# Two of the eight key tiles' maxima laid into the score banks by ScalarE instead of multiplied in by TensorE

## The reference

```python
attn = jnp.einsum('bhqd,bhkd->bhqk', attn_q, attn_k) / math.sqrt(HD)
rel = (pos[None, :] - pos[:, None]).astype(x.dtype)
attn = attn + slopes[None, :, None, None] * rel[None, None, :, :]
attn = jax.nn.softmax(attn, axis=-1)
out = jnp.einsum('bhqk,bhkd->bhqd', attn, v)
```

## Time and profile before

| What | Value |
|---|---|
| median of 3 runs | 1104.69 us (1103.84 to 1105.12) |
| the profiled execution's own time | 1104.65 us |
| its span in the trace | 1102.8 us |
| TensorE busy | 1050.2 us, 95% of the span |
| VectorE busy | 825.1 us, 75% |
| GpSimd busy | 791.3 us, 72% |
| ScalarE busy | 712.9 us, 65% |
| global attention, first to last score product | 103.5 to 684.6 us of the span |

### The profile page before, as it was taken

One profiled execution on the slowest core, in us unless ns is written; L12 is line 12 of the kernel. 1 busy time (PEld: TensorE's weight loads), 2 busy tenths in 40 slices (PEclk: granted clock), 3 DMA queues, 4 the chain that ended last, 5 costly groups with the idle time before them and its releaser, 6 DMA issues. The chain is left out here.

```text
span 1102.8 us, 23118 instructions
## 1 busy us (share of the span) xinstructions
PE 1050.2 (95%) x8304; PEld 652.5 (59%) x8304; DVE 825.1 (75%) x1490; ACT 712.9 (65%) x1285; POOL 791.3 (72%) x542
## 2 busy tenths in 40 slices
PE   7985999999999999999999999889999897999988
PEld 3662555555555555555555555766777694777778
DVE  7975676767666666666666664689999689999876
ACT  3663676767676767676767665048877656888754
POOL 3873678778777877787778778679996338666526
PEclk9995999999999999999999999999999999999999
DMA  8697123204132232141322100101111100111111
GB/s 267 212 285 235 37 50 78 58 30 107 30 79 58 59 78 59 31 106 34 83 57 51 39 13 21 39 11 33 34 44 35 25 2 17 36 35 34 36 29 34
DMA packets 71744, 71.70 MB, mean 65 GB/s; under 512 B 31396, under 2 KB 56528, under 8 KB 71632
## 3 DMA queue, kind: packets, MB, share of 16 engines
q1 hardware_dynamic: 71632, 70.23, 24.0%
HBM read 44.65 MB, written 15.85 MB: 55 GB/s over the span
## 5 line engine op out<-in xcount | busy, mean ns | idle before, releaser
L923 DVE CUSTOM_DVE_ANT_0 junk<-psum,alibi 128x1024 bf16<-128x1024 f32 x256 | 312.7, 1222 | 194.2 <-PE psum L995 186.5
L888 ACT ACTIVATE E<-psum,keybias_sb 128x1024 f32<-128x1024 f32 x256 | 277.8, 1112 | 189.6 <-PE psum L1019 175.2
L805 POOL TENSOR_TENSOR sum_p<-sum_p,E 128x1024 f32<-128x1024 f32 x96 | 232.8, 2425 | 84.4 <-ACT E L888 79.8
L1031 PE MATMUL psum<-E,V 128*64 128x512 f32 x1024 | 248.0, 605 | 0.0
L995 PE MATMUL psum<-KH,QH 64*128 64x512 f32 x512 | 118.6, 459 | 11.6 <-PEq L292 6.0
L1031 PEld LDWEIGHTS psum<-E,V 128*64 128x64 f32 x1024 | 62.1, 136 | 112.3 <-issue 106.4
L995 PEld LDWEIGHTS psum<-KH,QH 64*128 64x128 f32 x512 | 49.4, 189 | 120.5 <-DVE M L923 84.2
L1019 PE MATMUL psum<-QH,KH 64*128 64x512 f32 x512 | 102.2, 395 | 2.2 <-DMA QM<-mrow 2.2
L813 POOL TENSOR_TENSOR sum_p<-sum_p,xpos_sb 128x1024 f32<-128x1024 f32 x32 | 76.5, 2390 | 38.2 <-DVE xpos_sb L933 38.2
L1019 PE MATMUL psum<-QL,KH 64*128 64x512 f32 x512 | 101.5, 392 | 0.0
L1019 PE MATMUL psum<-QH,KL 64*128 64x512 f32 x512 | 101.4, 392 | 0.0
(11 more groups left out here) (155 smaller groups left out, 2087.2 us busy)
## 6 DMA issues: line engine op xcount, KB each, us to landing
qa_scratch<-tQ SPq DMA_DIRECT2D x8, 1024.0 KB, 5.3
QH<-qa_scratch SPq DMA_DIRECT2D x32, 256.0 KB, 3.6
QH<-qa_scratch SPq DMA_DIRECT2D x64, 128.0 KB, 3.5
vp_att<-v_att SPq DMA_DIRECT2D x64, 128.0 KB, 2.3
XF<-inverse_scratch SPq DMA_DIRECT2D x30, 256.0 KB, 3.4
KH<-k_scratch SPq DMA_DIRECT2D x16, 256.0 KB, 4.2
KL<-k_scratch SPq DMA_DIRECT2D x16, 256.0 KB, 5.2
v_scratch<-v_sb SPq DMA_DIRECT2D x16, 128.0 KB, 4.5
```

The source lines that it names most:

```text
L805: pool.tensor_tensor(sum_p[:, s, :], first, E[:, k % 4, :], ALU.add)\
L888: act.activation(E[:, k % 4, :], scores(k % 2), ACT.Exp, bias=kb).then_inc(exp_done, 1)
L923: dve.tensor_tensor_reduce(junk[:, :], banks(max_bank(i, k), 2), alibi[:, s, :], -1.0, BIG, ALU.add, ALU.min, M[:, s, k:k + 1]).then_inc(m ...
L1031: last = pe.matmul(banks(6 + i % 2)[HD * ch:HD * ch + HD, :], V[:, g, k, :], E[:, k % 4, ch * 512:(ch + 1) * 512], start=(k == 0), stop=(k ...
```

## The change

In heads 1 to 30, for key tiles 5 and 7 (`LAID`), the fourth product is left out. In its place ScalarE copies a wide tile, `m_wide` (128 partitions that each hold all 1024 negated maxima of the head), into the score banks, right after the exponential of tile `k - 2` (`lay_m`); TensorE waits for that copy (`laid_done`), and all three products that are left accumulate onto it. The wide tile is made by two new DMAs for each such head: `put_m` writes `mrow` to DRAM, `widen_m` reads the row back into all partitions. `put_m` stands between `load_m` and `widen_inverse` in SyncE's queue, `widen_m` after `spread_denominators`. `m_wide` lies in the first half of `XF`; for that `den_sb` moves to a buffer of its own, and the users of this half of `XF` at the end of the stage wait for the last laying. `take_m` also waits for `put_m` of the row's use two heads ago. `alibi_row` moves from after tile 5 to after tile 7.

```diff
@@ -96,6 +96,7 @@
     k_d = nc.dram_tensor("k_scratch", (B, KV // 2, 2, P, TB, P), F32, kind="Internal").ap()
     v_d = nc.dram_tensor("v_scratch", (B, P, TB, KW), F32, kind="Internal").ap()
     inv_d = nc.dram_tensor("inverse_scratch", (2, N), F32, kind="Internal").ap()
+    m_d = nc.dram_tensor("maxima_scratch", (2, N), F32, kind="Internal").ap()
 
     with ExitStack() as whole:
         whole.enter_context(nc.allow_non_contiguous_dma(reason="a few columns of biases"))
@@ -664,9 +665,10 @@
 
             sum_p = sb("sum_p", [P, 2, N])
             sum_d = xpos[:, 1].rearrange("p t s q d -> p (t s q d)").rearrange("p (s n) -> p s n", n=N)
-            den_sb = XF[:, 0:DQ // P, :].rearrange("p t d -> p (t d)")
+            den_sb = sb("den_sb", [P, DQ])
             inv_wide = XF[:, TB:T, :].rearrange("p t d -> p (t d)")
             inv_rows = XF[:, 4:8, :].rearrange("p t d -> p (t d)").rearrange("p (s n) -> p s n", n=DQ)
+            m_wide = XF[:, 0:TB, :].rearrange("p t d -> p (t d)")
             den8 = sb("den8", [P, 2, TB])
             inv8 = sb("inv8", [P, 2, TB])
             ones = sb("ones_m", [P, 32])
@@ -694,11 +696,24 @@
             inv_done = sem("inv_done")
             wide_mm = sem("wide_mm")
             o_done = sem("o_done")
+            m_out = sem("m_out")
+            m_in = sem("m_in")
+            laid_done = sem("laid_done")
             NP, ND = len(POOL_SUMS), len(DVE_SUMS) - 1
 
 
             def scores(s):
                 return banks(2 * s, 2)
+
+            LAID = (5, 7)
+
+            def is_laid(i, k):
+
+                return k in LAID and 0 < i < HEADS - 1
+
+            def laid_before(i):
+
+                return len(LAID) * (min(i, HEADS - 1) - 1)
 
             LEAD = TB + TB // 2
 
@@ -724,6 +739,18 @@
                         for ch in range(2):
                             sp.dma_start(QM[HD * ch:HD * ch + 1, s, :].bitcast(F32).rearrange("p (t c) -> p t c", c=P),
                                          mrow[TB // 2 * ch:TB // 2 * (ch + 1), s, :].bitcast(F32)).then_inc(ld_m[s], 16)
+
+                    def put_m(i, s):
+
+                        need(sp, mrow_done, i + 1)
+                        need(sp, m_in, 16 * (i - 2))
+                        sp.dma_start(m_d[s].rearrange("(t c) -> t c", c=P), mrow[:, s, :].bitcast(F32)).then_inc(m_out, 16)
+
+                    def widen_m(i, s):
+
+                        need(sp, m_out, 16 * i)
+                        need(sp, laid_done, laid_before(i))
+                        sp.dma_start(m_wide, m_d[s].partition_broadcast(P)).then_inc(m_in, 16)
 
                     def spread_denominators(i, s):
 
@@ -769,10 +796,14 @@
                             put_inverse(i - 2, i % 2)
                         if i + 1 < HEADS:
                             load_m(i + 1, (i + 1) % 2)
+                        if i + 1 < HEADS - 1:
+                            put_m(i + 1, (i + 1) % 2)
                         if i > 1:
                             widen_inverse(i - 2, i % 2)
                         if 0 < i < HEADS - 1:
                             spread_denominators(i - 1, (i - 1) % 2)
+                        if i + 1 < HEADS - 1:
+                            widen_m(i + 1, (i + 1) % 2)
 
                     for i in range(HEADS):
                         head(i)
@@ -825,6 +856,7 @@
                         head(i)
                     divide(HEADS // 2 - 2)
                     second_rstd(pool, 0)
+                    pool.wait_ge(laid_done, laid_before(HEADS - 1))
                     for t in range(NORMED):
                         modulate_out(pool, t)
                         shifted_out(pool, t)
@@ -866,7 +898,14 @@
                     def take_m(i, s):
                         need(act, m_turned, i + 1)
                         need(act, ld_m[s], 32 * (i // 2))
+                        need(act, m_out, 16 * min(i - 2, HEADS - 2))
                         act.activation(mrow[:, s, :], small_bank(i)[0:TB, DQ:DQ + P], ACT.Copy).then_inc(mrow_done, 1)
+
+                    def lay_m(i, k):
+
+                        need(act, m_in, 16 * i)
+                        need(act, exp_done, TB * i + k - 1)
+                        act.activation(scores(k % 2), m_wide, ACT.Copy).then_inc(laid_done, 1)
 
                     def head(i):
                         for k in range(TB):
@@ -886,9 +925,11 @@
                                 need(act, sum_d_done, ND * j + max(1, DVE_SUMS.index(old)))
                             kb = keybias[:, i, k:k + 1]
                             act.activation(E[:, k % 4, :], scores(k % 2), ACT.Exp, bias=kb).then_inc(exp_done, 1)
+                            if is_laid(i, k + 2):
+                                lay_m(i, k + 2)
                             if k == 4 and i + 3 < HEADS:
                                 high_q(i + 3, (i + 3) % 4)
-                            if k == 5 and i + 3 < HEADS:
+                            if k == 7 and i + 3 < HEADS:
                                 alibi_row(i + 3, (i + 3) % 2)
                             if k == 1 and i >= 1 and i + 2 < HEADS:
                                 round_q(i + 2, (i + 2) % 4)
@@ -941,6 +982,7 @@
                     def invert_rows(i):
 
                         need(dve, den_mm, i + 1)
+                        need(dve, laid_done, laid_before(HEADS - 1))
                         dve.reciprocal(inv_rows[:, i % 2, :], small_bank(i)[:, 0:DQ]).then_inc(inv_done, 1)
 
                     def divide_last():
@@ -1013,11 +1055,16 @@
                         keys = slice(k * P, (k + 1) * P)
                         terms = ((KH[:, g, keys], QH[:, s]), (KH[:, g, keys], QL[:, s]), (KL[:, g, keys], QH[:, s]),
                                  (one_rows[:, :], QM[:, i % 2]))
-                        for n, (key, query) in enumerate(terms):
+                        laid = is_laid(i, k)
+                        if laid:
+                            need(pe, laid_done, laid_before(i) + LAID.index(k) + 1)
+                        count = len(terms) - laid
+                        for n, (key, query) in enumerate(terms[:count]):
                             for ch in range(2):
                                 rows = slice(HD * ch, HD * ch + HD)
                                 last = pe.matmul(scores(k % 2)[:, ch * 512:(ch + 1) * 512], key[rows], query[rows, 0:512],
-                                                 start=(n == 0), stop=(n == len(terms) - 1))
+                                                 start=(n == 0 and not laid), stop=(n == count - 1),
+                                                 skip_group_check=laid)
                         last.then_inc(qk_done, 1)
 
                     def pv_step(i, k):
```

## The result

The changed kernel takes 1097.88 us (median of 5 runs, 1096.36 to 1101.35) against 1105.12 us for the kernel before (5 runs, 1103.84 to 1109.75): a ratio of 0.9929, 95% interval 0.9907 to 0.9951. It is faster by 7 us where 13.9 were forecast, and lies above the forecast's range (1089.8 to 1092.3) and above the wider one (to 1096.0). The profiled execution took 1097.59 us, against 1104.65.

The account below looks back on a forecast made before the run. The prediction took TensorE's own work to bound the global attention: 60 products at 0.2325 us make 13.95 us, and 1104.65 less that gives 1090.7, forecast as 1090.8 us. Its own range was 1089.8 to 1092.3, the wider one 1089.2 to 1096.0.

Parts of the forecast that it names:

- What bounds the kernel: Global attention: TensorE is full and waits for nobody; each of 60 dropped products gains 0.2325 us, 13.95 us in all.
- The fourth rival: TensorE's dropped products: each is worth its whole length, 60 x 0.390 = 23.4 us, giving 1081.3 us; chance 0.02.
- ScalarE, its layings, SyncE's queue: Layings of 1.15 us end 0.8 us before TensorE needs them; the wide copy lands in 3.2 us, 7.1 free.
- a disturbed TensorE: Second rival: ScalarE's PSUM writes slow TensorE during 66 us of layings; at half pace 1123.8 us; chance 0.06.
- a late copy: Third rival: the wide copy to all partitions lands after 7.6 us; at 9 us, 1147.7 us; chance 0.02.
- VectorE, the nearest neighbour: TensorE's maxima waiting for VectorE's reads: 0.17 us left at one, 0.09 at a head's last, 0.03 beyond the signal.
- stays covered too: GpSimd's waits for VectorE's sum, 1.2 us each, outlast the 0.46 us by which a head shortens.
- The first rival: New TensorE waits, for VectorE at the last maximum or for laying signals, eat 6 us: 1096.8 us; chance 0.12.
- The fifth: Rival: nothing changes because something read as loose, such as VectorE's ring of maxima, sets the pace: 1104.7 us; chance 0.03.
- the slower side: Whole kernel: the time comes out slower than before by more than about 0.2%; chance 0.07.
- The third rival: The wide copy lands late, deciding at 7.6 us; at 9 us each head loses 1.9 us: 1147.7 us; chance 0.02.
- Extra checks at a tile's border taken at nothing: TensorE's extra semaphore check at tile borders costs nothing, at most 0.06 us each, 3.6 us.

Follow-up runs that it names:

- The experiment with only the new work: Changed kernel with layings, DMAs and waits kept, but all four products in every tile, overwriting what was laid: 1105.83 us, ratio 0.9990 to the kernel before.
- making the low part small: Changed kernel with GpSimd's low part of the queries computed for 8 of 512 columns: 1092.49 us, ratio 0.9877; same edit in the kernel before: 1106.17 us, 0.9997.

## Why the prediction was wrong

**What bounds the kernel: right.** TensorE's list sets the pace, and a product is worth the distance of starts. The 0.2325 us measured 0.214 and 0.224 us (table above): 13.1 us for 60, in place of 13.95. The 0.214 is the low end: in the seven other traces without tile 5's product tile 3 to tile 4 takes 1.945 to 1.955 us, 0.23 less than before, and tile 4 to tile 5 takes 3.04. The two stretches together shrink by 0.16 to 0.17 us in all eight. The fourth rival, a product's whole length, is refuted.

**ScalarE, its layings, SyncE's queue: right.** The wide copy lands 1.4 us later than taken, inside the allowance. The experiment with only the new work puts their price at 0.2 us of stage. The rivals of a disturbed TensorE and a late copy are refuted: in that experiment ScalarE laid 60 tiles in other banks than TensorE's, and a head kept its 18.29 us. The prediction read "the cost is nothing" out of the Trainium skill, "PSUM — Partial Sum Buffer", Specifications (TRN2). That sentence is about VectorE and ScalarE side by side. The trace agrees with it for ScalarE's writes beside VectorE's reads (1.03 us and 1.21 to 1.23 us each), but it says nothing of TensorE, so only the experiment shows that.

**VectorE, the nearest neighbour: the step that failed.** It checked the maxima of tiles 6 and 7 (VectorE's reads of tiles 5 and 6) and found 0.03 us beyond the signal for the last one. These held: the stretch to tile 6's maximum lost its product whole (0.224 us), and tile 6 to tile 7 takes 2.197 us after, 2.195 before. It left out the border of the heads, where VectorE's sum of tile 7 stands ahead of its maximum of tile 0 and TensorE's of tile 1 waits for that; no product is removed there. But only 0.11 us stood there before the change, 0.06 of them the signal, and the step took VectorE's times as fixed. The sum's 1.42 us is not, it is 1.22 us of work and 0.20 us of waiting for GpSimd. What moves it is not the border's own distance but that between tile 6's exponential, which releases GpSimd, and tile 7's maximum, which precedes VectorE's sum. Tile 7's product lay between the two. Its removal brings them 0.23 us closer, the overlap grows from 0.34 to 0.56 us, the sum from 1.42 to 1.64, and the gap is used up: 0.177 us a head, 5.3 us, shown by making the low part small (5.1 us of stage back) and by laying tile 3 in place of tile 7.

**The same step left out a second place, tile 4's maximum.** Tile 5's product is removed ahead of it, so TensorE comes 0.23 us earlier, while VectorE's read of tile 3 stays where it was. Before, that read ended 0.43 us ahead of TensorE's matmul. That looks ample, as the prediction's 0.40 us at tile 6 did, but what waits is the weights, and they load 0.23 us ahead of the matmul: 0.20 us stood there (407.42 to 407.62). The wait that opens costs 0.055 us a head by the table, 1.7 us, and 0.07 us by the seven other traces. At tile 6 the weights now start 0.053 us behind VectorE's read as well; that is just early enough and costs about 0.01 us.

**GpSimd "stays covered too": wrong in kind.** The prediction looked at whether GpSimd's waits were long enough, and not at when it runs. It is never late in the changed kernel; it is in the way.

**The first rival: right in kind, in the wrong place.** It named the last maximum of a head waiting for VectorE, which did not happen, and the signal of each laying, which costs nothing. A wait of TensorE for VectorE did take the gain, two maxima later. That the time fell into its span (chance 0.12), 1.1 us from its 1096.8, is luck: its 0.1 us at each of 60 tiles was none of the two waits that came. **The fifth** (nothing changes) and **the slower side** did not come. The third rival's sum counts 1.9 us a head from 7.1 us on, where its own threshold of 7.6 gives 1.4 and 1132.7 us; nothing else rests on it.

**Extra checks at a tile's border taken at nothing: right.** With the check for the laying in place and all products kept, a head took its 18.29 us. Without any check, the dropped products alone showed the same loss.

So 13.1 - 5.3 - 1.7 = 6.1 us by the two places, 6.7 by the head times, 7.1 by the stage. The 0.6 us between the first two are 0.02 us a head, spread over the other maxima; the last 0.4 us are not accounted for.

## What to carry to other kernels

When work is removed from the engine that sets the pace, check every wait of that engine on another, measured from the instruction that waits (here the weights, 0.23 us ahead of the matmul). And don't check only the steps whose distance shrinks: list every pair of operations of two other engines whose relative start shifts, and see whether they hold each other up when they overlap. A duration in a trace that is longer than the same operation elsewhere (1.42 against 1.22 us) is the sign of such a pair, and its length is not a constant. Of several equal pieces of work, remove the one that leaves such pairs apart: here tile 3 in place of tile 7 was worth 4 us more.

## What the runs showed of the hardware

VectorE's sum of two SBUF tiles and GpSimd's operations exclude each other: the one that starts second waits for the end of the first. VectorE's 128x1024 sum took 1.22 us alone, and with overlaps of 0.34, 0.56 and 1.78 us it took 1.42, 1.64 and 2.86, each time 1.22 plus the overlap less 0.14. The other way round it is the same: GpSimd's 128x1024 sums took 2.35 to 2.44 us alone, and the 348 in the twelve traces that started during a sum of VectorE's took 2.22 to 2.26 us plus the overlap. VectorE's maxima, with one input in PSUM and one in SBUF, kept 1.21 to 1.23 us whatever GpSimd did, in every one of the twelve traces. The Trainium skill says both: "SBUF — State Buffer", Who interferes with whom, has the pair of ports that VectorE and GpSimd share as an exclusive lock, taken by a VectorE instruction with two SBUF inputs against a GpSimd one that reads SBUF, and not by one with a single SBUF input. The trace agrees with each number here. Read beside the 1.42 us of the trace before, that rule would have told that 0.20 of them were a wait.

ScalarE's write of a 128x1024 tile from SBUF to PSUM took 1.03 us, and a head with two of them kept its 18.29 us. From the end of VectorE's read to the start of TensorE's weights it took 0.05 us where the weights carried the wait themselves, and 0.114 to 0.118 us at tile 4's maximum, where an instruction with the wait stood ahead of them.
